# A 64-state scan stage: sums in 64x64 tiles, carry copies on GpSimd, B row first, y a pair later

## What is computed

```python
u = (u0 - mu) * jax.lax.rsqrt(var + EPS) * gamma + beta       # u0: half of x @ W_in
dtbc = u @ W_dt + b_dt                                        # 8 columns, 64 of B, 64 of C
delta = jax.nn.softplus(dt_raw @ W_dtr + b_dtr)
deltaA = jnp.exp(delta[..., None] * A[None, None])
dBu = delta[..., None] * B_ssm[:, :, None, :] * u[..., None]
_, h = jax.lax.associative_scan(_scan_comb, (deltaA, dBu), axis=1)   # h = deltaA * h_before + dBu
y = jnp.einsum('bldn,bln->bld', h, C_ssm) + u * D_param
y = y.reshape(Bb, Hh, Ww, Cc) + xc                            # xc: a gated 3x3 depthwise convolution
return x + transpose(y @ W_out)
```

## Time and profile before

| | |
|---|---|
| median of 3 runs | 10609.8 us |
| profiled execution | 10616.9 us, span 10615.1 us |
| TensorE (matmul) busy | 9717.4 us, 92% |
| VectorE busy | 8515.8 us, 80% |
| ScalarE busy | 8057.9 us, 76% |
| GpSimd busy | 5905.9 us, 56% |
| the scan stage that changes | first scan 2838.8 us, last y 5945.1 us |

### The profile page before, as it was taken

How to read it: one execution, slowest core, us unless ns; L and a number is a source line. 1 busy time by engine, 2 the same in 40 slices (tenths; PEclk the granted TensorE clock), 3 DMA queues, 4 the chain that set the end, 5 groups by cost and what they waited for, 6 DMA issues and landing times. The chain is left out here.

```text
span 10615.1 us, 137498 instructions
## 1 busy us (share of the span) xinstructions
PE 9717.4 (92%) x45956; PEld 5177.6 (49%) x45956; DVE 8515.8 (80%) x8102; ACT 8057.9 (76%) x14637; POOL 5905.9 (56%) x2628
## 2 busy tenths in 40 slices
PE   9999999999899999999999999988888888888885
PEld 6767767677444444444444444433333333333332
DVE  7858858578599999999999411159999999999997
ACT  5646646466488888888888555579999998888885
POOL 0000000000288888888888300058989988889885
PEclk9999999999899999999999999989999999999997
DMA  1000000000145555545555100035555555555556
GB/s 41 0 1 0 0 0 0 0 0 0 61 173 175 175 175 174 177 174 174 176 174 177 66 8 8 8 120 184 186 184 179 187 182 189 184 186 188 183 187 220
DMA packets 335957, 1241.58 MB, mean 117 GB/s; under 512 B 38672, under 2 KB 38800, under 8 KB 331792
## 3 DMA queue, kind: packets, MB, share of 16 engines
q1 hardware_dynamic: 335472, 1235.51, 34.7%
HBM read 1145.18 MB, written 56.62 MB: 113 GB/s over the span
## 5 line engine op out<-in xcount | busy, mean ns | idle before, releaser
L951 POOL TENSOR_TENSOR l_hc<-l_h,l_hc 128x1024 f32<-128x1024 f32 x1024 | 2398.8, 2365 | 451.5 <-DVE l_h L1049 451.0
L1841 POOL TENSOR_TENSOR l_ring<-l_ring 128x1024 f32<-128x1024 f32 x1024 | 2429.7, 2397 | 347.4 <-DVE l_ring L1919 341.3
L1919 DVE TENSOR_TENSOR_SCAN l_ring<-l_ring,l_carry,l_ps 128x1024 f32<-128x1024 f32 x960 | 2200.1, 2333 | 1.3
L688 PE MATMUL l_ps<-l_hc,w_sb 128*128 128x512 f32 x4096 | 1936.4, 595 | 69.1 <-POOL l_hc L951 61.7
L1049 DVE TENSOR_TENSOR_SCAN l_h<-l_decay,l_carry,l_ps 128x1024 f32<-128x1024 f32 x768 | 1760.3, 2334 | 4.3 <-issue 0.4
L1545 PE MATMUL l_ps<-l_ring,w_sb 64*64 64x512 f32 x8192 | 1216.9, 667 | 343.0 <-POOL l_ring L1841 334.4
L116 POOL COPY l_qm<-l_q 128x128 f32 x128 | 82.7, 648 | 2576.4 <-PE l_ps L188 2179.5
L829 ACT ACTIVATE l_decay<-l_delta,w_sb 128x1024 f32<-128x1024 f32 x1024 | 1152.8, 1138 | 168.8 <-DVE l_h L1049 168.6
L1731 ACT ACTIVATE l_xt<-l_duT,l_BT 128x128 f32<-128x128 f32 x4096 | 1246.0, 388 | 0.0
L842 ACT ACTIVATE l_xt<-l_duT,l_BT 128x128 f32<-128x128 f32 x4096 | 1245.9, 388 | 0.0
L212 PE MATMUL l_ps<-l_attnT,l_vT 128*128 128x128 f32 x8192 | 1095.7, 277 | 1.3 <-ACT l_attnT L283 1.3
(11 more groups left out here) (233 smaller groups left out, 15001.6 us busy)
## 6 DMA issues: line engine op xcount, KB each, us to landing
l_hc<-l_rows_dram SPq DMA_DIRECT2D x1024, 512.0 KB, 3.7
l_ring<-l_rows_dram SPq DMA_DIRECT2D x1024, 512.0 KB, 4.8
l_crossed<-l_delta SPq DMA_DIRECT2D x128, 256.0 KB, 5.3
l_gate_dram<-l_gate SPq DMA_DIRECT2D x32, 512.0 KB, 7.1
l_recon_dram<-l_recon SPq DMA_DIRECT2D x32, 512.0 KB, 5.4
l_gate<-l_gate_dram SPq DMA_DIRECT2D x32, 512.0 KB, 6.0
l_xw<-x_dram SPq DMA_DIRECT2D x30, 513.5 KB, 7.3
x_dram<-x SPq DMA_DIRECT2D x16, 512.0 KB, 2.6
```

Source lines behind the costliest of these rows:

```text
L688: ins = nc.tensor.matmul(y_sum[:, half(j)], ident, hc[:, unit % CS, half(j)], start=q == 0, stop=q == S1 - 1)
L951: nc.gpsimd.tensor_tensor(hc[:, unit % CS, :], h[:, unit % HS, :], hc[:, unit % CS, :], ALU.mult).then_inc(hc_done, 1)
L1841: nc.gpsimd.tensor_tensor(hc[:, unit % CS, :], h[:, unit % HS, :], hc[:, unit % CS, :], ALU.mult).then_inc(hc_done, 1)
L1919: nc.vector.tensor_tensor_scan(h[:, unit % HS, order], decay[:, unit % DS, order], x_now[:, order], before, ALU.mult, ALU.add).then_inc(sc ...
```

## The change

In the 64-state layer alone:

- The sums of a pair are made together, in two phases of four 64x64 matmuls: the four tiles of the array take the lower and the upper half of the even and the odd state. The odd state of a pair is held with its two halves of channels exchanged. To that end the odd decays are made from `crossed`, a copy of delta with exchanged halves, which SyncE makes with two DMAs a chunk; A and du's transposes are exchanged in the same way.
- On TensorE the next B row comes right behind the turn-back, ahead of the sums. The first phase of the sum waits for both products of its pair. The pair's convolution and preparation follow, and then the second phase, which waits for the first to be complete.
- The carry copies move from VectorE to GpSimd, each in front of its unit's product.
- y of the chunk before is read between the two scans of pair 1, instead of behind those of pair 0. The preparation's first pieces move back: u from pairs 0 and 1 to 2 and 3, its squares to 3, the variance to 5, the root to 6 and 7.
- `part` moves into `z2`, which makes room for `crossed`; two waits guard it.

```diff
+            def cross_delta(K):
+                sp.wait_ge(delta_ready, K + 1)
+                at_least(sp, decay_ready, S1 * K)
+                for side in range(2):
+                    sp.dma_start(crossed[64 * side:64 * side + 64, :],
+                                 delta[64 - 64 * side:128 - 64 * side, K % 2, :]).then_inc(crossed_in, 16)
             store_rows(0)
+            cross_delta(0)
...
+                    if q == 62 and K + 1 < NCH:
+                        cross_delta(K + 1)
...
-            def add_state(unit):
-                K, q = divmod(unit, S1)
-                if q == 0:
-                    at_least(pe, y_out, K)
-                pe.wait_ge(hc_done, unit + 1)
-                for j in range(2):
-                    ins = nc.tensor.matmul(y_sum[:, half(j)], ident, hc[:, unit % CS, half(j)], start=q == 0,
-                                           stop=q == S1 - 1)
-                ins.then_inc(sum_mm, 1)
+            def add_pair(P, phase):
+                K, k = divmod(P, PAIRS)
+                if phase == 0:
+                    if k == 0:
+                        at_least(pe, y_out, K)
+                    pe.wait_ge(hc_done, 2 * P + 2)
+                    at_least(pe, sum_mm, 2 * P)
+                else:
+                    pe.wait_ge(first_half_mm, P + 1)
+                lower, upper = slice(0, 64), slice(64, 128)
+                for own, other, j in ((lower, upper, phase), (upper, lower, 1 - phase)):
+                    for odd, to in enumerate((own, other)):
+                        ins = nc.tensor.matmul(ps[to, 4 + j, :], ident[own, own], hc[own, (2 * P + odd) % CS, half(j)],
+                                               start=k == 0 and phase == 0, stop=k == PAIRS - 1 and phase == 1)
+                if phase == 1:
+                    ins.then_inc(sum_mm, 2)
+                else:
+                    ins.then_inc(first_half_mm, 1)
...
                     turn_back(P)
+                    if P + 1 < NCH * PAIRS:
+                        broadcast_B(P + 1, p if k + 1 < PAIRS else 1 - p)
                     if P:
-                        add_state(2 * P - 2)
+                        add_pair(P - 1, 0)
...
-                    if P + 1 < NCH * PAIRS:
-                        broadcast_B(P + 1, p if k + 1 < PAIRS else 1 - p)
                     if P:
-                        add_state(2 * P - 1)
+                        add_pair(P - 1, 1)
...
+                if q == 1:
+                    act.wait_ge(crossed_in, 32 * K + 32)
-                nc.scalar.activation(decay[:, unit % DS, :], delta[:, p, :], ACT.Exp,
+                nc.scalar.activation(decay[:, unit % DS, :], crossed[:] if q % 2 else delta[:, p, :], ACT.Exp,
...
             def product(unit):
+                K, q = divmod(unit, S1)
+                pool.wait_ge(scan_done, unit + 1)
+                if K % NC < NC - 1:
+                    nc.gpsimd.tensor_copy(carry[:, q:q + 1], h[:, unit % HS, CH - 1:CH]).then_inc(kept, 1)
                 pool.wait_ge(c_in[unit % CS], 16 * (unit // CS) + 16)
-                pool.wait_ge(scan_done, unit + 1)
...
-                        if k == 1:
+                        if k == 3:
                             squares(K + 1, 1 - p)
...
                     scan(P, 0)
+                    if k == 1 and K:
+                        add_y(K - 1, 1 - p)
                     scan(P, 1)
-                    if k == 0 and K:
-                        add_y(K - 1, 1 - p)
...
-                    if K % NC < NC - 1:
-                        keep(2 * P)
-                        keep(2 * P + 1)
```

More of the change, by code:

```diff
@@ L482, in scan_layer @@
         delta = sb("delta", [128, 2, CH])
+        crossed = sb("crossed", [128, CH])
         du = sb("du", [128, 2, CH])
@@ L490, in scan_layer @@
         rest = sb("rest", [DT_AT + R1, CH])
-        part = sb("part", [PARTS * SEL, CH], BF16)
         z1, z2 = sb("z1", [128, CH]), sb("z2", [128, CH])
         z3, rows_sb = usq, z1[0:S1, :]
+        part = z2[0:PARTS * SEL, 0:CH // 2].bitcast(BF16)
         carry = sb("carry", [128, S1])
@@ L720, in _ @@
                     if K + 1 < NCH:
-                        if k < 2:
-                            prep_u(K + 1, k)
-                        if k == 4:
+                        if k in (2, 3):
+                            prep_u(K + 1, k - 2)
+                        if k == 5:
                             prep_var(K + 1)
-                        if k in (5, 6):
-                            prep_rstd(K + 1, k - 5)
+                        if k in (6, 7):
+                            prep_rstd(K + 1, k - 6)
                         if k in (8, 9):
@@ L738, in _ @@
                         project(K - 1, k - 21)
-                    if P + 1 < NCH * PAIRS:
-                        broadcast_B(P + 1, p if k + 1 < PAIRS else 1 - p)
                     if P:
-                        add_state(2 * P - 1)
-            for unit in range(NCH * S1 - 2, NCH * S1):
-                add_state(unit)
+                        add_pair(P - 1, 1)
+            for phase in range(2):
+                add_pair(NCH * PAIRS - 1, phase)
             for j in range(2):
@@ L776, in split_high @@
                 act.wait_ge(bdt_out, 2 * K + 2)
-                nc.scalar.activation(part[:], rest[0:PARTS * SEL, :], ACT.Identity,
+                at_least(act, low_ready, 2 * K)
+                nc.scalar.activation(part, rest[0:PARTS * SEL, :], ACT.Identity,
                                      scale=w[0:PARTS * SEL, L1_AT["below_top"]][:, 0:1]).then_inc(part_ready, 1)
@@ L884, in _ @@
                     if K + 1 < NCH:
[L885 to L887 removed]
+                        if k in (2, 3):
+                            u_copy(K + 1, 1 - p, k - 2)
+                        if k == 5:
                             roots(K + 1)
[L889 to L890 removed]
+                        if k in (7, 8):
+                            add_beta(K + 1, 1 - p, k - 7)
                         if k in (8, 9):
@@ L918, in split_rest @@
                 own = rest[0:PARTS * SEL, :]
-                nc.gpsimd.tensor_tensor(own, own, part[:], ALU.subtract).then_inc(rest_ready, 1)
+                nc.gpsimd.tensor_tensor(own, own, part, ALU.subtract).then_inc(rest_ready, 1)
             def split_last(K, p):
                 pool.wait_ge(part_ready, 2 * K + 2)
-                nc.gpsimd.tensor_tensor(stack[:, p, :], rest[0:PARTS * SEL, :], part[:],
+                nc.gpsimd.tensor_tensor(stack[:, p, :], rest[0:PARTS * SEL, :], part,
                                         ALU.subtract).then_inc(stack_ready, 1)
@@ L1050, in scan @@
                                              before, ALU.mult, ALU.add).then_inc(scan_done, 1)
[L1052 to L1055, removed]
             dve.wait_ge(weights_in, 32)
@@ L2125, in layer1_arrays @@
                ("out_w", 0, W_out), ("ident", 0, _np.eye(128)), ("ones", 0, _np.ones((128, 1))),
-               ("A", 0, A_log[:, by_unit]), ("below_top", 0, below_top), ("minus_one", 0, _np.full((128, 1), -1)),
+               ("A", 0, _np.where(_np.arange(S1) % 2, _np.roll(A_log[:, by_unit], 64, 0), A_log[:, by_unit])),
+               ("below_top", 0, below_top), ("minus_one", 0, _np.full((128, 1), -1)),
                ("bdt_b", 0, column(_np.concatenate([b_dt[even_B]] * PARTS + [b_dt[:R1]]))),
```

12 lines of the change are left out of this document (7 added, 5 removed).

## The result

The change makes the kernel slower by a little: 10649.2 us median (10642.2 to 10655.9) against 10609.2, a ratio of 1.0036 with a 95% interval of 1.0025 to 1.0047. The forecast was 10622, its own range 10595 to 10650 and the wide one 10580 to 10670: the result is 27 us above the forecast and 0.8 us inside the upper end of its own range.

A forecast was written before the change was run, and what follows sets the result against it. VectorE was taken as the bound, with TensorE brushing it. From 10616.9: -47.5 + 15 (early stall) + 23 (late) + 20 (clock) + 1 (prologue) = +12, so 10629, or 10622 against the median; own range 10595 to 10650, wide 10580 to 10670.

The forecast's parts named there:

- Same: Outcome within 0.2% of the kernel before, about 21 us; chance 0.42.
- What goes: Scan stage: B row stalls 25.2 us, stall before y 11.3, VectorE's carry copies 11; together 47.5 us saved.
- the seven places: Pairs 1, 5, 6, 7, 13, 21, 22, where a carry copy delays VectorE by 0.13 us; 11 us over 12 chunks.
- The cap: Limit on any gain, as VectorE's plain pair stays at 5.74 us: no faster than 10562 us.
- buy nothing beyond the stalls above: 64x64 tiles give TensorE 1.6 us per pair, but with VectorE the bound only the removed stalls are gained.
- GpSimd's lag: Early and late pairs: GpSimd's products end late, each delayed further by a one-column copy of cost c, taken as 0.12 us.
- The early stall: Pair 5: VectorE waits for the variance, 0.6 + 5c a chunk, 15 us in all; slow clock adds 14 x 1.0.
- The late stalls: Pair 24's odd input comes late, 0.6 + 9c a chunk, taking in pairs 21 and 22: 23 us; clock adds 15 x 0.4.
- the crossing: SyncE's two DMAs of delta per chunk, issued in pair 30, land with 5 us of cover; put at nothing.
- little comes back: Rival: the stalls go and the two new chains cost only 25 us; 10588 us, chance 0.24.
- GpSimd as the bound: Rival: one-column copies decide from 0.38 us on; 10664 us at 0.50 us a copy, chance 0.12.
- The clock at full size: Rival: scan stage loses as much to TensorE's slow clock as the later tiled stage, 177 us; 10740 us, chance 0.10.

The follow-up runs named there:

- e8: e7 with the carry copies on VectorE again, behind the even input's product: 10562.8 us, ratio 0.9957.
- e7: Changed kernel, convolution and preparation right behind the turn-back, GpSimd's tap addition in pair 8, softplus and delta extras spread over pairs 18 to 24, transposes later: 10560.6 us.
- b1: Kernel before, with the next pair's B row sent right behind the turn-back, ahead of the first half's sum: 10722.8 us, ratio 1.0106.
- e2: Changed kernel with three unused 128x512 filler matmuls in TensorE's two pauses of pair 5: 10640.1 us, ratio 1.0027.
- b3: Kernel before with only GpSimd's softplus and delta pieces spread over pairs 18, 20, 22 and 24, transposes a pair later: 10591.2 us, ratio 0.9980.
- b4: Kernel before with three more 8-column VectorE operations per chunk, in pairs 8, 9 and 11, results unused: 10661.8 us in one run.
- e4: Changed kernel with all convolution and preparation of a pair right behind the turn-back, ahead of B row and sums: 10608.8 us, ratio 1.0004.

## Why the prediction was right or wrong

**The number.** The median lies 0.8 us inside the forecast's own range and well inside the wide one. Part of that is luck: three terms were short by 37 us, and a gain of 9 us that the forecast didn't have made up for some of it. "Same", within 0.2% of before, had the largest chance and did not come; it is 0.36% slower.

**What goes.** The stalls for the B row and before y went as said. For the copies e8 is the test without the other stalls: six of the seven places cost 0.09 us a chunk each, 7.6 us in 14 chunks for the 9 to 10 forecast, but pair 5 gives 3.4 back, and the ratio shows no difference. The cap (10562) was right: e7, which has nearly no stall, ran in 10560.6. The statement that the 64x64 tiles "buy nothing beyond the stalls above" hides what b1 showed, that without them the row in front costs 1.06%.

**GpSimd's lag** was right to the tenth. The copy costs 0.11 us for 0.12 taken. Pair 4's products were to end 3.4 + 5c = 4.0 us into pair 5; in chunk 2 the sum that waits for them starts 3267.53 - 3263.47 = 4.06 us in.

**The early stall is the term that was farthest off**, and in it the clock. Without the clock it was put at 1.2 us, with it at 2.2 ("a chance of 0.7, 14 x 1.0"); it is 3.3 in the mean, and 3.88 in chunk 2. Sum and variance took 1.92 + 3.5 us there for the 1.0 + 1.7 in the sum, 2.7 more. The ratio of 1.5 came from eight records that had run at both levels in part; the whole chain ran at the lower one, and the pause in front is there in every chunk. e2 is the proof: with the clock back the wait is 19.4 us, for the 15 of the chain without it, and the clock's part is 28.5, for 14. Together this is 47.9 us for 29, 19 of the 27 by which the forecast was short.

**The late stalls** were to be one in pair 24 that takes in the others, 29 us with the clock. They came in four pairs: 19 (10.7 us in 15 chunks), 21 (4.1 in 6), 22 (11.4 in 14) and 24 (8.4 in 6). Against e7, after loses 0.82 us in pairs 19 and 20 and 1.83 in pairs 21 to 25: 2.65 x 14 = 37 us. Most of it is there at full clock as well: pairs 21 to 25 took 31.7 us in the mean of the three chunks with 1.00 in pairs 20 to 24, and 32.3 in the eight others that keep a carry. The first of the four is the wait for decays, 10.7 us, put at 0 to 0.8 a chunk and inside the late stall; it is 0.7 and stands alone; a wait for a decay was one of the forecast's own signs of being wrong. b3 and e7 show that these pairs hang on GpSimd, as the chain said.

**Put at nothing, the crossing** cost VectorE nothing: no wait of a scan for a decay stands outside pair 19. But it had no cover on ScalarE, which waits for it at the first odd decay of each chunk (3500 to 4500, five chunks):

```profile
L855 ACT ACTIVATE l_decay<-l_crossed,w_sb 128x1024 f32<-128x1024 f32 x163 | 185.2, 1136 | 13.3 <-DMA l_crossed<-l_delta 12.9 <-DVE l_h L1078 0.4
```

**Not seen:** pairs 6 and 7 lose 0.73 us a chunk against e7, 10 us (the wait for the reciprocal root's product, 10.2). And on the other side the Newton steps: before spends 784 ns in the median on the first, after 166, some 9 us less, since in after GpSimd's products have ended before it starts, behind VectorE's stall. 19 + 8 + 10 - 9 is 28, near the 27.

**Rivals.** The first ("little comes back") is what e7 is, not the change. GpSimd as the bound needed copies of 0.38 us; they cost 0.11. The clock at full size (10740) did not come; the part of it that did, came mostly in the early chain. "TensorE is busy 700 to 760" was 819: its records are longer at the lower level. The clock, 0.96, was inside 0.90 to 0.97. The chances gave 0.42 to the same and 0.34 to slower; slower it was.

## What to carry to other kernels

Where an engine gets lighter work and a new wait, price the chain behind the wait at the lower clock level in full, if that chain ends at the engine that bounds; where it doesn't, the same low clock was free here. Before an order is changed, follow each of its waits to who holds the buffer: a piece moved in front can pause its engine once per iteration. When a stall is removed, ask what it had kept apart; here it had kept VectorE's small operations away from GpSimd's long ones.

## What the runs showed of the hardware

VectorE operations of 8 fp32 columns that read only SBUF waited for GpSimd's running instruction to end: 1.40 us in b4, up to 2.36 in e4, for 0.17 alone. The same size with a PSUM input took 0.16, and products of 1024 columns with a PSUM operand took 1.21 us with GpSimd running or not, scans 2.35 for 2.32. In e7 this still costs 1.0 us a chunk (1174 ns for 168). Reading the variance from PSUM in that step may avoid it; that wasn't tried.
